# Two heads by half the tokens: new stacks, new key chunks and no clearing product in a two-attention decoder layer

## The reference

```python
x = _layernorm(x + self_attention(x))        # 16 heads of width 8, one shared key and value head
x = _layernorm(x + cross_attention(x, ctx))  # 16 heads of width 8, keys and values from 6404 context rows, masked
x = _layernorm(x + experts(x))               # router over 8 experts, the best one, weighted
# attention: scores = Q K^T / sqrt(8); softmax over the keys; out = attn V; out @ Wo + bo
```

## Time and profile before

| | us |
|---|---|
| median of 3 runs | 506.13 (505.16 to 506.8) |
| span of the profiled execution | 505.4 |
| TensorE busy | 482.0 (95%) |
| VectorE busy | 419.7 (83%) |
| ScalarE busy | 368.0 (73%) |
| GpSimd busy | 209.5 (41%) |

### The profile page before, as it was taken

One profiled execution on the slowest core, in us unless ns is written; L12 is line 12 of the kernel. 1 busy time (PEld: TensorE's weight loads), 2 busy tenths in 40 slices (PEclk: granted clock), 3 DMA queues, 4 the chain that ended last, 5 costly groups with the idle time before them and its releaser, 6 DMA issues.

```text
span 505.4 us, 13819 instructions
## 1 busy us (share of the span) xinstructions
PE 482.0 (95%) x4122; PEld 197.3 (39%) x4122; DVE 419.7 (83%) x612; ACT 368.0 (73%) x718; POOL 209.5 (41%) x316
## 2 busy tenths in 40 slices
PE   7999999999999999987999999999999999999983
PEld 2433333333333344632344444444444444433641
DVE  5999999999999926668699989999899899831766
ACT  6358888888888875441678877877878887787263
POOL 4825755885469900132233323333233332320045
PEclk9899999999999999999799999999999999999997
DMA  4859864875453014524133110111111111010101
GB/s 116 350 147 305 280 219 166 298 259 194 167 173 137 12 54 123 161 62 121 42 71 81 41 40 26 40 37 30 38 32 40 40 40 40 27 40 22 43 1 45
DMA packets 21772, 52.58 MB, mean 104 GB/s; under 512 B 5021, under 2 KB 13375, under 8 KB 19649
## 3 DMA queue, kind: packets, MB, share of 16 engines
q1 hardware_dynamic: 18461, 22.46, 16.8%
q0 software_dynamic: 2304, 28.84, 15.4%
q10 hardware_dynamic: 932, 0.37, 0.3%
HBM read 42.10 MB, written 8.94 MB: 101 GB/s over the span
## 4 chain that ended last, share of the span: by engine, by line
PE 81%; DVE 9%; ACT 5%; issue 3%; DMA 1%; SPq 0%; DVEq 0%; POOL 0%; ACTq 0%; POOLq 0%
PE O L1321 32%; PE ST L1555 15%; PE RT L1527 10%; PE ST L1352 10%; PE RT L1338 5%; DVE mxs L786 3%; ACT prob L1102 2%; PE O L1292 1%; DVE mxc L937 1%; PE RT L1231 1%; ACT Vx L1180 1%; PE O L1317 1%; PE RT L1464 1%; ACT prob L1141 1%; PE RT L1679 1%
## 5 line engine op out<-in xcount | busy, mean ns | idle before, releaser
L937 DVE TENSOR_REDUCE mxc<-RT 128x1024 f32 (+1 forms) x192 | 196.1, 1045 | 23.4 <-PE RT L1527 18.9
L1141 ACT ACTIVATE prob<-ST 128x512 f32<-128x512 f32 x320 | 172.4, 596 | 38.7 <-PE ST L1555 36.8
L1102 ACT ACTIVATE prob<-ST 128x512 f32<-128x512 f32 x256 | 138.6, 597 | 24.7 <-PE ST L1352 14.1
L786 DVE TENSOR_REDUCE mxs<-RT 128x2 f32<-128x1024 f32 x128 | 152.7, 1224 | 2.8 <-PE RT L1338 0.6
L1527 PE MATMUL RT<-Kr,Qs 64*128 64x128 f32 (+1 forms) x512 | 121.8, 375 | 2.7 <-DVEq L924 1.2
L1555 PE MATMUL ST<-Qs,Kc 64*128 64x512 f32 x320 | 122.3, 458 | 2.0 <-DMA Qs<-qd_x 1.4
L1321 PE MATMUL O<-prob,vst 128*9 128x256 f32 x1280 | 100.3, 385 | 1.7 <-ACT prob L1141 1.3
L1338 PE MATMUL RT<-Kself,Qs 64*128 64x512 f32 x256 | 89.6, 454 | 1.8 <-DVE Kself L753 0.9
L1352 PE MATMUL ST<-Qs,Kself 64*128 64x512 f32 x256 | 91.2, 450 | 0.0
L1321 PE MATMUL O<-prob,Vs 128*9 128x256 f32 x1024 | 79.3, 381 | 1.5 <-ACT prob L1102 0.7
L1555 PEld LDWEIGHTS ST<-Qs,Kc 64*128 64x128 f32 x320 | 54.5, 187 | 61.2 <-issue 31.6
(11 more groups left out here) (232 smaller groups left out, 355.4 us busy)
## 6 DMA issues: line engine op xcount, KB each, us to landing
big<-in_mask POOLq DMA_DIRECT2D x16, 1760.0 KB, 7.3
big<-kd SPq DMA_DIRECT2D x66, 80.0 KB
od_s<-osb SPq DMA_DIRECT2D x14, 128.0 KB, 1.9
od_x<-osb SPq DMA_DIRECT2D x14, 128.0 KB, 1.8
Qs<-qd_s SPq DMA_DIRECT2D x12, 128.0 KB, 6.3
Qs<-qd_x SPq DMA_DIRECT2D x12, 128.0 KB, 3.8
qd_s<-Vx SPq DMA_DIRECT2D x2, 512.0 KB, 4.8
qd_x<-big SPq DMA_DIRECT2D x2, 512.0 KB, 4.5
```

The source lines that it names most:

```text
L786: v.tensor_reduce(mxs[:, h % 2, c2, :].rearrange("p (f t) -> p f t", f=2)[:, :, q], RT[r % 2][:, :].rearrange("p (f k) -> p f k", f=2), AX ...
L937: v.tensor_reduce(o, src, AX.X, ALU.max).then_inc(S("x_row_free"), 1)
L1102: nc.scalar.activation(prob[:, c % SLOTS, k * HALF:(k + 1) * HALF], ST[(2 * c + k) % 3][:, :], ACT.Exp) \
L1141: nc.scalar.activation(prob[:, b, (k % 2) * HALF:(k % 2 + 1) * HALF], ST[BANK[k]][:, :], ACT.Exp) \
```

## The change

It is a rewrite of the program around a new unit, with the same products.

- **Stacks.** A unit is two heads by half the tokens: partitions 0 to 63 are one head, 64 to 127 the next, both for the same 512 tokens. Units 0 to 7 are the 16 heads of tokens 0 to 511, units 8 to 15 those of tokens 512 to 1023. The value products take a different head's values for each half (`add_values`).
- **Keys** are one block of 1024 and then chunks of 256: here one chunk, 1280 keys as before. A cross unit has 10 blocks and 10 row fills, 8 of 512 keys and 2 of two token tiles by 256 keys.
- **The first value product** of a unit is issued with start=True and waits for `o_copied`; `clear_o` and its zeros are gone.
- **One list of steps.** Steps 0 to 127 are self attention, 128 to 287 cross attention (`X(j, b)` is block b of cross unit j); row products run 15 steps ahead all through. Other work stands at fixed steps of the list: tokens 0 to 511 are projected, normalised and made into queries at steps 72 to 88, and 512 to 1023 at X(1,0) to X(2,4); keys and values of the block of 1024 at steps 90 to 96; counting the live keys at 98 and 100; the chunk at 104; the first half's second normalisation, router and two of its expert groups from X(9,0) on.
- **Keys go straight to Kr and Kc**: GpSimd issues the loads (`load_rows`, `load_cols`); the ring and its copies are gone.
- **Square roots** that fall inside the streams are powers on GpSimd (`inverse_std`).
- **The end** (`finish`) has the second half of the tokens and what is left of the first half's experts.

```diff
-PAIR = 640
-NBLK = PAIR // P
-NP = -(-KEYS // PAIR)
-KPAD = NP * PAIR
+KS, KC = 1024, 256
+SBLK, CBLK = KS // P, KC // P
+NBLK = SBLK + CBLK
+NP = -(-(KEYS - KS) // KC)
+KPAD = KS + NP * KC
...
+SELF = UNITS * SELF_U
+STEPS = SELF + UNITS * NBLK
...
+RT_JOBS = {74: ("s0 spread",), 77: ("s0 y",), 90: ("k",), 98: ("count",), 100: ("flags",), KV - 1: ("km",),
+           X(1, 0): ("s1 spread",), X(1, 4): ("s1 y",), X(9, 0): ("x0 spread",), X(9, 4): ("x0 y",),
+           X(10, 4): ("x0 logits",), X(14, 6): ("e0",), X(15, 1): ("e1",),
...
-            def clear_o(a, g):
-                if g:
-                    pe.wait_ge(S(a + "_o_copied"), g)
-
-                mmul(O[:, 0:256 + P], zrow[:, 0:P], zrow[:, :], start=True, stop=False, skip_group_check=True)
-
-            def add_values(v, slot):
+            def add_values(v, slot, G=None):
+
+                if G:
+                    pe.wait_ge(S("o_copied"), G)
                 for q in range(4):
-                    mm = mmul(O[32 * q:32 * q + VW, 0:256], v, prob[:, slot, q * 256:(q + 1) * 256],
-                              start=False, stop=False, skip_group_check=True)
+                    mm = mmul(O[32 * q:32 * q + VW, 0:256], v[q // 2], prob[:, slot, q * 256:(q + 1) * 256],
+                              start=G is not None, stop=False, skip_group_check=True)
                 return mm
...
+                def load_rows(U, part):
+                    w = (slice(0, 512), slice(512, KS), slice(KS, KUSE))[part]
...
+                    for f in range(2):
+                        r = PRODUCTS[f]
+                        pool.dma_start(Kr[r:r + PROD, w].bitcast(F32), head_rows(U, f)[:, w]).then_inc(S(f"kr{part}"), 16)
...
+            def row_products(o, U, u, f, gen):
+
+                if u < SRU:
+                    parts = [(u % 4, slice(512 * (u // 4), 512 * (u // 4) + 512), 0)]
+                else:
+                    parts = [(2 * (u - SRU) + k, slice(KS, KUSE), KC * k) for k in range(2)]
```

More of the change, by code:

```diff
@@ L41 @@
 DIRECT = 2
[L42 to L47, removed]
+UNITS = 16
 SELF_U = 8
-LA = 7
+RU = 10
+SRU = 8
+LEAD = 15
 SLOTS = 5
-HALFT = KPAD // 2
 E = 8
@@ new lines, in _ @@
+            for h in range(2):
+                for k in range(2):
+                    sp.wait_ge(S(("q_high", "q_low")[k]), h + 1)
+                    load(qd["s"][k].rearrange("d h q -> h d q")[:, :, tokens(h)],
+                         (qhigh.bitcast(F32), qlow)[k][:, tokens(h)], "q_out")
+                if h == 0:
+                    sp.wait_ge(S("q_out"), 32)
+                    queries(DIRECT, 4, "q_in0")
+            max_rows(0)
+            queries(4, 8, "q_in")
+            for h in range(UNITS):
@@ L325, in _ @@
-                    load(wo_x[:, :], t["wo_x"], "in_w")
                     load(wr[:, :], t["wr"], "in_w")
@@ L638, in _ @@
+            pool.wait_ge(S("kd_out"), 64)
+            pool.wait_ge(S("st_free"), number(ST_AT, "v1"))
+            before = steps[0]
+            with pool.If(slow == 0):
+                usual()
             with pool.Else():
-                stream(True)
-            step = 5
+                steps[0] = before
+                any_keys()
             def add(o, a, b):
-                g_.tensor_tensor(o, a, b, ALU.add).then_inc(S("pool_step"), 1)
-            def four_experts(q0, q1):
-                pool.wait_ge(S("y_part"), 4 * q1)
+                step(g_.tensor_tensor(o, a, b, ALU.add))
@@ new lines, in residual, with normalised @@
+            def residual(a, ph):
+                w = tiles(ph)
+                bank = ready(f"{a}{ph} y")
+                dve.wait_ge(S("x_bias"), 1 if a == "s" else 2 + ph)
+                freed(v.tensor_tensor(x[:, w, :], x[:, w, :], bank[:, 0:HALF].rearrange("p (t d) -> p t d", d=D), ALU.add))
+                dve.wait_ge(S("rt_free"), number(RT_AT, f"{a}{ph} y"))
+                statistics(ph, "var")
+            def normalised(o, ph, name):
+                for q in range(4 * ph, 4 * ph + 4):
@@ new lines, in _ @@
+            sums_back(4)
+            spread_rows("x", 1)
+            residual("x", 1)
+            dve.wait_ge(S("std"), 4)
+            ch(v.reciprocal(rstd[:, 4:8], rstd[:, 4:8]))
+            normalised(x, 1, "xn")
+            dve.wait_ge(S("bias_in"), 1)
+            statistics(0, "f_var")
+            router_max(1)
+            dve.wait_ge(S("f_std"), 1)
+            normalised(outs, 0, "out_done")
+            router_weights(1)
+            lower_experts(2)
+            lower_experts(3)
@@ L1243, in half_q0, with free @@
[L1243 to L1253 removed]
+            def free(kind, k):
+                name, base = FREED[kind]
+                pe.wait_ge(S(name), base + k + 1)
@@ new lines, in rt_place, with st_place @@
+            def rt_place(key, chunks=False):
+                kind, k, bank, prior = RT_AT[key]
+                if prior is not None and not (chunks and RT_AT[prior][0] != "rt"):
+                    free(*RT_AT[prior][0:2])
+                return RT[bank]
+            def st_place(key, chunks=False):
+                kind, k, bank, prior = ST_AT[key]
+                if prior is not None and not (chunks and ST_AT[prior][0] != "st"):
+                    free(*ST_AT[prior][0:2])
+                return ST[bank]
@@ L1722, in _ @@
+            with pe.If(slow == 0):
                 cross(False)
```

2217 lines of the change are left out of this document (1146 added, 1071 removed).

## The result

| | change | before | ratio, 95% interval |
|---|---|---|---|
| median of 6 runs each, us | 509.68 (508.78 to 511.93) | 506.34 (505.16 to 508.1) | 1.0067 [1.0041, 1.0092] |
| span of the profiled execution, us | 508.9 | 505.4 | |

The change is 0.7% slower than the kernel before. The prediction said 473.7 us, 457 to 490, and faster with a chance of 0.94: size and sign were wrong. (The change's executions took 1.6 to 1.7 us longer than their spans, where the prediction had added 0.7.)

What follows compares the result with a forecast made beforehand. It took TensorE to bound both attention streams. Self attention's end at 222.0 us, cross attention's terms to 440.0 and a 33 us tail gave 473.0, plus 0.7 for the median: 473.7 us, range 457 to 490.

Steps and rivals of the forecast that it cites:

- Self units 10.35, clear 0: Self attention: each unit still takes 10.35 us; removing the clear gains 0, as it lay under ScalarE's exponential.
- The clear in cross attention: Boundaries of cross attention: the clear stood in the open, the next column product issued 0.27 us after it.
- Cross units 12.95: Cross attention: 12.95 us a unit, from 10 steps of 1.21, boundary 0.65, and 0.1 for each of two steps.
- The hand-over, 6 us: Around step 104: stall of 3, chunk's load 2, register reads and branch 1; 6 us, bounds 0 and 20.
- the rival built on it: Hand-over: its waits run in series, 20 us in place of 6, total 487 us; chance 0.18.
- What comes into the streams: Jobs moved under attention: TensorE 11.8 us self, 6.6 cross; VectorE stalls 6 and 3.5; ScalarE copies 2 and 1.5; expert fills 1.
- The two expert fills: End of cross attention, where no row products are left: they add 1 us.
- Key loads on GpSimd counted 0: Ten small loads a unit: issues and copies take 6.9 of 12.95 us, so they are hidden and cost 0.
- none above 1.5 elsewhere: TensorE: a hole of 3 us around step 112, and no other above 1.5 us before the tail.
- The rival with 1.42 us an issue: GpSimd becomes the bound: from 1.42 us an issue the kernel is slower than before, 532 us at 1.6; chance 0.05.
- VectorE's stalls, 6 and 3.5: VectorE's longer jobs stall TensorE 6 us in self and 3.5 in cross attention, of 23 us of jobs.
- VectorE as the bound of the whole: VectorE's 23 us of jobs are added in full instead of 9.5, total 487 us; chance 0.12.

Runs made afterwards that it cites:

- e5: The change with the clearing product put back before each unit's first value product: 510.49 us, ratio 1.0065 to the kernel before.
- e6: The kernel before without its clearing product, the first value product of each head opening the bank: 507.17 us, ratio 1.0018.
- e8: The change with the edits of e1, e2 and e3, SP's maxima rows issued earlier (e4), and the first query gather in three parts: 483.30 us, ratio 0.9557.
- e2: The change with the split of a unit's maxima put before the normalisation's work in GpSimd's list: 500.35 us, ratio 0.9883.
- e1: The change with GpSimd's conversion of the mask counts waiting until VectorE has normalised the first half: 503.04 us, ratio 0.9957.
- e11: The change with GpSimd's conversion of the mask counts cut into eight pieces at its old place: 505.83 us, ratio 0.9983.
- e3: The change with the second half's stacked queries gathered in three parts over three cross units, not all at once: 503.39 us, ratio 0.9948.
- e7: The change with the edits of e1, e2 and e3 together: 487.94 us, ratio 0.9621 to the kernel before.
- e10: e8 with idle TensorE products added where TensorE waits in the tail: 482.18 us, ratio 0.9518 to the kernel before.
- e12: e8 with the idle products of e10 and the first half's steps 72 to 88 three steps later: 479.55 us, ratio 0.9473.
- e4: The change with SP issuing unit 9's maxima before the first half's sums and unit 12's before the key stores: 510.36 us, ratio 1.0070.

## Why the prediction was wrong

Its working, step by step:

- **Self units 10.35, clear 0**: right (e5). **The clear in cross attention**, which I had in the open: it is not, in either kernel (e6). A column product follows the zeros at once there, but without the zeros (e6) that product waits 0.20 us for an exponential.
- **Cross units 12.95**: 13.15. The plain step was 1.21 as taken; the 0.1 for each of the 256-key steps did not appear, and the boundary took 1.0 us instead of 0.65 (spacings of 1.70 and 1.74). 3 us in all.
- **The hand-over, 6 us, called the least known term**: less. At steps 102, 104 and 110 the spacings exceed the usual ones by 1.9, 0.7 and 0.3 us, the chunk's own products included, and the rival built on it fell. What I worked on most was not where the risk lay.
- **What comes into the streams**: the prices of the products and of VectorE's operations added up well. In e8, where most of the holes are gone, self attention spends 220.8 - 32.0 - 16 x 10.35 = 23.2 us on them, where the sum had 25.8; cross attention's units 16 to 30 hold 16.0 over 13.15 each, where it had 12.6. The two expert fills alone took 3.4 instead of 1. (One slip in the sum: eight value blocks at the row's rate are 2.0, not 1.8.)
- **Key loads on GpSimd counted 0, and "none above 1.5 elsewhere"**: here the prediction failed. An issue took 0.50 us (0.59 assumed), a 64 KB load landed in 2.1 us. (2.2 was the estimate from the Trainium skill, DMA: Bandwidth & Descriptors, "Anatomy of one DMA — SWDGE (gpsimd) path"; the trace agrees.) The rival with 1.42 us an issue was far off. But I asked only whether GpSimd has time in a unit (6.9 of 12.95 us), not what stands ahead of what in its list. The edit "square roots are powers on GpSimd" got no term at all. Its wait for statistics, and at one place the work on the new queries, in front of a 0.5 us split cost 9.3 us (e2).
- **VectorE's stalls, 6 and 3.5**: I priced its operations by rows of a stage in which GpSimd stood idle. Beside GpSimd's long conversion four of them took 7.5 us instead of 1.1, which cost 5.6 us (e1, e11).
- **SP's gathers counted nothing**: 1 MB each, they were costed neither as issues nor as traffic. The second made a key load 8 us late (e3, 6.0 us), the first and SP's order perhaps 3.2 more (e8, not clear of noise). The holes of e1, e2 and e3 together are 22.6 of the 35.9 us by which the span was missed (e7).
- **The clock**: every term assumed full speed. After the holes it was not granted, and in the tail, which I had built from rows of a tail with idle products (granted clock 1.00 from 476 to 488 us), it was 0.54 from 484 to 492 us. Idle products took 1.9 us off the tail of e8 (e10); the change's was 4.4 too long.

With the five edits the predicted curve is nearly there: 220.8 for 222.0 us, 444.9 for 440.0, span 481.2 for 473.0. So the gain of the rewrite exists, some 23 us with five edits and 27 with the two more of e12; as written, the kernel gives all of it back in waits that come from the order of its lists, from the gathers and from what GpSimd's long instructions hold. Of the rivals, VectorE as the bound of the whole is out: e2's gap was not filled by it and e7's gains add. At steps 71 and 72 alone, in e4 and e8, it is what TensorE waits for. GpSimd's came nearest, but by its pace, where it was its order. Between e12's span of 480.1 and 473.0 lie 6.0 us in cross attention (3 of them the boundaries, 2.4 the expert fills) and 1.4 in the tail. The end of self attention was met in e8 in part by luck: the hand-over took some 3 us less than its 6, and the hole at steps 71 and 72 (2.59 and 5.25 us), whose held-off copy and slow clock the sum did not have, took that up.

## What to carry to other kernels

When work is moved under a dense stream, the sum of its costs is the easy half. For every short item that the bound engine waits for, read the list of the engine that makes it: what stands ahead, and what does that wait for. The urgent short item goes first, bulk transfers go in parts, and no long GpSimd instruction runs over VectorE's copies and tensor_scalar operations. Two holes of which one hides the other must be closed together, or closing one may show nothing.

## What was not expected of the hardware

- A 128x128 tensor_scalar of VectorE took up to 5.87 us instead of 0.34, held off for the length of one GpSimd instruction, and a copy of 22 elements 1.68 to 1.83 instead of 0.18; the reductions, which read PSUM, took 1.21 to 1.23 beside the same kinds of instruction.
- A load of 80 KB landed after 10.31 us instead of 2.2, behind 1 MB that another engine had begun to issue 1.9 us before it.
- TensorE's granted clock fell behind waits of 1.80, 2.52 and 2.54 us and stayed at half for another 3 us or so of full work: 9.9 us for 6.9 of waits. Behind a wait of 2.10 us elsewhere it did not fall; in e8 it fell behind waits of 0.89 and 0.52 us (steps 71 and 72).
- A product of 384 columns more or less at each of 32 boundaries changed nothing that can be measured.
